# Softmax denominators in a causal latent-attention kernel: from eight fp32 transposes per query tile to a block-transposed reduction and one 16-column product

## Chip, core and metric

The kernel runs on one core of one Trainium2 chip. The metric is the device time of one execution in microseconds (us). The changed program computes the same outputs from the same inputs. Engine names are those of the profile: PE is TensorE (PEld its weight loads), DVE VectorE, ACT ScalarE, POOL GpSimd, SP the engine that issues most DMAs.

## What is computed

One sequence of 2048 tokens of width 512 goes through a latent attention with 16 heads, a residual and a layer norm, then one linear layer with a second residual and layer norm. The part that matters here, from the reference:

```python
scores = jnp.einsum('bhqd,bhkd->bhqk', q_full, k_full) * scale
scores = jnp.where(causal, -jnp.inf, scores)
attn = jax.nn.softmax(scores.astype(jnp.float32), axis=-1).astype(q_full.dtype)
out = jnp.einsum('bhqk,bhkd->bhqd', attn, v)
out = out.transpose(0, 2, 1, 3).reshape(b, s, H * DV)
return out @ w_o.T
```

The change concerns the denominator of the softmax: for every query and head the sum of the exponentials over all keys up to the query.

## The kernel before

**Tiling.** The 16 heads are four groups of four. Within a group the 2048 queries are 16 tiles of 128. That makes 64 iterations `it`, each for one group and one query tile (128 queries by 4 heads are 512 columns). Iteration `it` has `keys(it)` key tiles, 1 to 16 of them, because of causality; over all iterations there are 544. Two query tiles that lie side by side are one after the other (a pair), the one with more keys first; the pairs follow `PAIR_ORDER`, so the first iterations of a group have 14, 13, 2, 1, 16, 15, 4, 3, 12, 11, 6, 5, 8, 7, 10 and 9 key tiles.

**One key tile.** Scores are held with keys on partitions and (head, query) along the free dimension, 128x512. For each key tile:

- PE: `scores`, five 512-column matmuls (line 1464) into one of two banks;
- ACT: copy of the scores to a ring of 24 slots in SBUF (line 1606); the masked first tile is written by DVE instead (line 1847);
- DVE: running maximum `max` over the key tiles (line 1858); it releases the bank for the scores two tiles later;
- DVE: `shift` by the spread maximum (line 1873); ACT: `exp` (line 1611) and rounding to the high part `hi` (line 1618); POOL: the low part `lo` (line 1730);
- DVE: `sum`, the running sum TOTAL of the exponentials in a PSUM bank (line 1882 copies the first tile there, line 1885 adds the others);
- PE: `values`, three 512-column matmuls (lines 1494, 1495 and 1497) into the bank OUT; the third waits for `lo`.

The exponentials of a tile are handled some six slots after its scores, so the end of one iteration lies beside the scores of a later one. A slot is one `scores` and one `values` on PE.

**The end of an iteration before the change.** TOTAL holds, for each of 128 partitions, one partial sum per (head, query). ACT copies it to SBUF (`copy_sum`, line 1630), PE transposes it in four 128x128 pieces (`turn_sum`, line 1505), DVE reduces along the free dimension to 128x4 and takes the reciprocal (`reduce_sum`, lines 1889 and 1892). PE then transposes four broadcast columns, which puts the inverse of each (head, query) on all 128 partitions (`spread_sum`, line 1513). DVE multiplies the values by it (`normalise`, line 1897), ACT and POOL round the result to two parts (`o_hi` line 1636, `o_lo` line 1735), and PE multiplies by the output weights in twelve 512-column matmuls (`y`, line 1527). DVE adds that to the sum of the output (`add_y`, line 1836).

**What sets the order.** `timetable()` gives each step a slot and a phase within it, `readers()` puts the readers of a step one slot later, and `plan()` sorts them, pulling a step forward where another needs it. Every engine works through the one list `STEPS` in that order. `turn_sum`, `spread_sum`, `turn_max`, `y`, and the projections `q` and `pe` of the next pair of query tiles share three PSUM banks (`AUX`), in turns. With `e` the slot of an iteration's last values:

```python
        yield e, COPIES, ("copy_sum", it)
        yield e + 1, COPIES, ("copy_out", it)
        yield e, USE_AT, ("turn_sum", it)
        yield e + 3, USE_AT, ("spread_sum", it)
        yield e + 5, USE_AT, ("y", it)
```

The readers of `spread_sum`, which are `normalise`, `o_hi` and `o_lo`, so stand in slot e + 4, ahead of the copy of scores and of `max` of that slot. "Boundary 16" below is the end of iteration 16, and so on.

Behind iteration 58 the second layer norm and the linear layer are mixed in (lines 1535, 1547, 1902 to 1941). Ahead of the attention there is a preparation of some 150 us.

Of the kernel before, what the change touches and what calls it, by code (L numbers as in the profile page):

```python
# [15 lines left out]
P = 128  # L16
# [753 lines left out]
def timetable():  # L770

    for it in range(N_ITER):
# [55 lines left out]
def readers(use):  # L828
# [30 lines left out]

def waits_for(step):  # L860
# [9 lines left out]
    elif what == "max":  # L870
        yield ("scores", it, *rest)
        if number(it, *rest) >= RING:
            yield ("lo", *previous(it, *rest, RING))
            yield ("sum", *previous(it, *rest, RING))
# [14 lines left out]
    elif what == "sum":  # L889
        yield ("exp", it, *rest)  # L890
        if it and rest[0] == 0:
            yield ("copy_sum", it - 1)
# [10 lines left out]
    elif what == "copy_sum":  # L903
        yield ("sum", *last_tile(it))
        if it:
            yield ("turn_sum", it - 1)
# [6 lines left out]
    elif what == "turn_sum":  # L913
        yield ("copy_sum", it)
    elif what == "reduce_sum":
        yield ("turn_sum", it)
        if it >= 2:
            yield ("spread_sum", it - 2)
    elif what == "spread_sum":
        yield ("reduce_sum", it)  # L920
# [96 lines left out]
AUX_USES = ("q", "pe", "y", "turn_max", "turn_sum", "spread_sum", "turn", "linear")  # L1017
# [72 lines left out]
def attention_phase(nc, m, block, x, bias, out):  # L1090


    with ExitStack() as ctx:
# [13 lines left out]
        total = sb("total", [P, 512])  # L1107
# [5 lines left out]
        sums = sb("sums", [P, 4, HG])  # L1113
# [41 lines left out]
        sum_copied = sem("sum_copied")  # L1155
        sum_turned = sem("sum_turned")
        sum_done = sem("sum_done")
# [47 lines left out]
        def by_head(view):  # L1205

            return view.rearrange("p (h n) -> p h n", h=HG)

# [176 lines left out]
        def _(pe):  # L1385
            def wait_read(u):
# [9 lines left out]
                elif u[0] == "turn_sum":  # L1396
                    pe.wait_ge(sum_done, u[1] + 1)
# [157 lines left out]
            for what, *at in STEPS:  # L1555
# [10 lines left out]
                elif what == "turn_sum":  # L1566
                    turn_sum(*at)
                elif what == "spread_sum":
                    spread_sum(*at)
# [12 lines left out]
        def _(act):  # L1582
# [12 lines left out]
            def copy_scores(it, t):  # L1595
# [6 lines left out]
                if n >= RING:  # L1602

                    act.wait_ge(p_lo, n - RING + 1)
                    act.wait_ge(summed, n - RING + 1)
# [19 lines left out]

            def copy_sum(it):
                act.wait_ge(summed, finished(it))
                if it:
                    act.wait_ge(sum_turned, it)
                nc.scalar.copy(total[:, :], TOTAL).then_inc(sum_copied, 1)  # L1630
# [36 lines left out]
            for what, *at in STEPS:  # L1667
# [20 lines left out]
                elif what == "copy_sum":  # L1688
                    copy_sum(*at)
# [104 lines left out]
        def _(dve):  # L1794
# [80 lines left out]
            def add_up(it, t):  # L1875
                n = number(it, t)
                dve.wait_ge(exp_done, n + 1)
                if t == 0:
                    if it:

                        dve.wait_ge(sum_copied, it)
                    nc.vector.tensor_copy(TOTAL, slot(n)).then_inc(summed, 1)
                else:
# [148 lines left out]
```

## Time and profile before

| what | value |
|---|---|
| time, median of 3 runs | 1715.34 us (1714.08 to 1717.51) |
| span of the profiled execution | 1714.7 us |
| PE busy | 1679.9 us, 98% |
| PEld busy | 1395.8 us, 81% |
| DVE busy | 1380.5 us, 81% |
| ACT busy | 1120.8 us, 65% |
| POOL busy | 979.7 us, 57% |
| granted TensorE clock, mean | 0.999 |

The span runs from the first to the last instruction of one profiled execution; its own time is not recorded apart from it. The median of the runs is 0.6 us longer than the span. Busy time of an engine is the time in which at least one of its instructions is under way. Matmuls overlap, so what one costs is read from the distance between starts, not from its duration.

### The profile page before, as it was taken

Reading aid. Unit: us, or ns where it says so; the run is one execution under the profiler, and the core shown is the slowest. Engines: PE = TensorE matmul, PEld = TensorE weight load, DVE = VectorE, ACT = ScalarE, POOL = GpSimd, SP = SyncE. Lnnn points to the kernel's source line nnn. Section 1 sums busy time; section 2 is a strip of 40 time slices with the busy share of each in tenths; the row PEclk is TensorE's granted clock in tenths of the full one; section 3 lists DMA queues with packets and bytes.
Section 4 is the critical chain, followed back from the end, with each engine's and each line's share of the span. In section 5 each row is a group of like instructions: output and inputs, shape, how many; then the busy total and the mean of one; then the engine's idle time right before and its main releaser. Section 6 shows DMA issues by size and latency. Waiting matters only on the chain.

```text
span 1714.7 us, 28541 instructions
## 1 busy us (share of the span) xinstructions
PE 1679.9 (98%) x8789; PEld 1395.8 (81%) x8789; DVE 1380.5 (81%) x2493; ACT 1120.8 (65%) x2128; POOL 979.7 (57%) x937
## 2 busy tenths in 40 slices
PE   7999999999999999999999999999999999999997
PEld 5567888888888888888888888888888888888775
DVE  3665788888888887878788888888888888888984
ACT  3564676666666676666677666766667777676774
POOL 4333465565555555655566555555556665556785
PEclk9999999999999999999999999999999999999999
DMA  7984322212321412223211413123123111111422
GB/s 204 367 330 136 105 68 62 87 56 88 110 80 37 144 36 81 69 80 117 81 62 44 142 50 92 51 80 114 62 66 105 56 57 62 50 44 44 136 92 80
DMA packets 112175, 164.03 MB, mean 96 GB/s; under 512 B 13600, under 2 KB 83488, under 8 KB 109984
## 3 DMA queue, kind: packets, MB, share of 16 engines
q1 hardware_dynamic: 105296, 125.86, 22.9%
q0 software_dynamic: 4864, 16.26, 3.0%
q10 hardware_dynamic: 1872, 20.19, 2.9%
q8 instruction: 68, 1.11, 0.3%
q14 instruction: 75, 0.61, 0.1%
HBM read 101.19 MB, written 61.08 MB: 95 GB/s over the span
## 4 chain that ended last, share of the span: by engine, by line
PE 89%; POOL 3%; DVE 3%; issue 2%; DMA 1%; ACT 1%; DVEq 0%; SPq 0%; ACTq 0%; POOLq 0%
PE rows L1464 35%; PE bank L1494 7%; PE bank L1497 7%; PE bank L1495 7%; PE rows L1527 7%; PE rows L1427 5%; PE bank L1527 3%; PE rows L392 2%; PE rows L1440 2%; PE bank L1427 2%; PE bank L1484 2%; PE bank L1440 1%; POOL split_p L1730 1%; PE rows L1473 1%; PE rows L1505 1%
## 5 line engine op out<-in xcount | busy, mean ns | idle before, releaser
L1730 POOL TENSOR_TENSOR split_p<-pool,split_p 128x512 fp32r<-128x512 f32 x544 | 703.3, 1294 | 503.2 <-ACT split_p L1618 503.1
L1464 PE MATMUL rows<-q_c,key_c 128*128 128x512 f32 x1632 | 477.0, 400 | 1.4 <-DVE top L1858 1.4
L1606 ACT COPY pool<-rows 128x512 f32<-128x512 f32 x480 | 281.8, 587 | 227.3 <-PE rows L1464 226.6
L1858 DVE TENSOR_TENSOR top<-rows,top 128x512 f32<-128x512 f32 x420 | 288.6, 687 | 124.5 <-ACT pool L1606 121.0
L1873 DVE TENSOR_TENSOR pool<-bank,pool 128x512 f32<-128x512 f32 x544 | 369.7, 680 | 19.8 <-PE bank L1484 19.8
L1611 ACT ACTIVATE pool<-pool 128x512 f32<-128x512 f32 x544 | 345.9, 636 | 18.1 <-DVE pool L1873 17.1
L1618 ACT CAST split_p<-pool 128x512 fp32r<-128x512 f32 x544 | 333.2, 612 | 16.7 <-PE bank L1497 16.7
L1464 PE MATMUL rows<-q_pe,key_pe 128*128 128x512 f32 x1088 | 337.1, 391 | 0.4 <-DMA q_pe<-pe_dram 0.4
L1885 DVE TENSOR_TENSOR bank<-bank,pool 128x512 f32<-128x512 f32 x480 | 330.9, 689 | 0.0
L1464 PEld LDWEIGHTS rows<-q_c,key_c 128*128 128x128 f32 x1632 | 288.0, 189 | 50.0 <-DVE top L1858 5.0
L1464 PEld LDWEIGHTS rows<-q_pe,key_pe 128*128 128x128 f32 x1088 | 204.2, 188 | 46.2 <-DMA q_pe<-pe_dram 0.9
L1497 PE MATMUL bank<-split_p,val 128*128 128x512 f32 x544 | 213.7, 393 | 2.9 <-POOL split_p L1730 2.7
L1494 PE MATMUL bank<-split_p,val 128*128 128x512 f32 x544 | 214.0, 393 | 1.5 <-ACT o_sum L1624 1.0
L1495 PE MATMUL bank<-split_p,val 128*128 128x512 f32 x544 | 212.3, 390 | 0.0
L1527 PE MATMUL rows<-wo,o_t 128*128 128x512 f32 x528 | 127.3, 390 | 0.4 <-ACT o_t L1636 0.4
L1497 PEld LDWEIGHTS bank<-split_p,val 128*128 128x128 f32 x544 | 102.1, 188 | 29.0 <-POOL split_p L1730 7.4
L1494 PEld LDWEIGHTS bank<-split_p,val 128*128 128x128 f32 x544 | 102.1, 188 | 25.9 <-ACT o_sum L1624 3.4
L1735 POOL TENSOR_TENSOR o_t<-o_sum,o_t 128x512 fp32r<-128x512 f32 x64 | 83.0, 1296 | 69.8 <-ACT o_t L1636 69.8
L1495 PEld LDWEIGHTS bank<-split_p,val 128*128 128x128 f32 x544 | 102.2, 188 | 21.2
L1527 PEld LDWEIGHTS rows<-wo,o_t 128*128 128x128 f32 x528 | 98.9, 188 | 21.7 <-issue 1.2
L1636 ACT CAST o_t<-o_sum 128x512 fp32r<-128x512 f32 x64 | 39.7, 621 | 111.4 <-DVE o_sum L1897 97.2
L1427 PE MATMUL rows<-cq,wq 128*128 128x256 f32 x612 | 80.1, 285 | 0.3 <-DVE key_pe L611 0.3
(193 smaller groups left out, 2101.9 us busy)
## 6 DMA issues: line engine op xcount, KB each, us to landing
q_pe<-pe_dram SPq DMA_DIRECT2D x128, 128.0 KB, 2.6
y_dram<-y SPq DMA_DIRECT2D x62, 256.0 KB, 2.1
cq<-cq_dram SPq DMA_DIRECT2D x19, 768.0 KB, 4.9
y<-y_dram SPq DMA_DIRECT2D x48, 256.0 KB, 3.0
pe_dram<-by_sin SPq DMA_DIRECT2D x32, 256.0 KB, 2.1
pe_dram<-by_cos SPq DMA_DIRECT2D x32, 256.0 KB, 2.2
cq_more<-cq_dram SPq DMA_DIRECT2D x10, 768.0 KB, 4.9
table<-table_dram SPq DMA_DIRECT2D x56, 128.0 KB, 2.7
```

Of the source, the lines that this page charges most:

```text
L1464: mm = pe.matmul(by_head(out), k, q, start=(z == 0), stop=(z == 4))
L1494: pe.matmul(OUT, m.val[:, 0, j, :], split_p[:, n % 2, 0, :], start=(t == 0), stop=False)
L1495: pe.matmul(OUT, m.val[:, 1, j, :], split_p[:, n % 2, 0, :], start=False, stop=False)
L1497: pe.matmul(OUT, m.val[:, 0, j, :], split_p[:, n % 2, 1, :], start=False, stop=(t == keys(it) - 1)).then_inc(values_done, 1)
L1527: mm = pe.matmul(aux(u), o_t[:, a, h * P:h * P + P], m.wo[:, b, h, :], start=(n == 0), stop=(n == 3 * HG - 1))
L1606: nc.scalar.copy(slot(n), SCORES[n % N_SCORES]).then_inc(scores_copied, 1)
L1611: nc.scalar.activation(slot(n), slot(n), ACT.Exp).then_inc(exp_done, 1)
L1618: nc.scalar.copy(split_p[:, n % 2, 0, :], slot(n)).then_inc(p_hi, 1)
L1730: nc.gpsimd.tensor_tensor(split_p[:, n % 2, 1, :], slot(n), stored(split_p[:, n % 2, 0, :]), ALU.subtract).then_inc(p_lo, 1)
L1858: nc.vector.tensor_tensor(out, SCORES[n % N_SCORES], slot(number(it, 0)) if t == 1 else out, ALU.max).then_inc(scores_maxed, 1)
L1873: nc.vector.tensor_tensor(slot(n), MAXES, slot(n), ALU.add).then_inc(shifted, 1)
L1885: nc.vector.tensor_tensor(TOTAL, TOTAL, slot(n), ALU.add).then_inc(summed, 1)
```

## The change

The partial sums are now reduced by DVE straight from PSUM with a transposing reduction: within each block of 32 partitions by 32 columns it transposes and then sums, so 128x512 becomes 128x16 (`reduce_sum`). Each 32-partition group then holds sums over its own 32 key rows. A 128x128 matrix `fold` of repeated 32x32 identities adds the four groups in one fp32 product of 16 columns on PE (`fold_sum`). DVE takes the reciprocal of those 16 columns, and transposes them, each broadcast to 32 columns, in 32x32 blocks into the same PSUM bank, which puts the inverse of each (head, query) on all partitions (`spread_sum`, now a step of DVE). `copy_sum`, `turn_sum` and the old `spread_sum` are gone. The first exponential tile is no longer copied to TOTAL; the add of the second tile reads both. Where an iteration has one key tile, the copy stays. `fold` is built once by two DVE instructions. `spread_sum`, `normalise`, `o_hi` and `o_lo` are readers of `fold_sum`, and `y` is at e + 3.

```diff
         e = last_value(it)
         yield last_slot(it) + 1, USE_AT, ("turn_max", it)
         yield value_slot(it, 0) - 3, SPREAD, ("spread_max", it)
-        yield e, COPIES, ("copy_sum", it)
+        yield e, COPIES, ("reduce_sum", it)
         yield e + 1, COPIES, ("copy_out", it)
-        yield e, USE_AT, ("turn_sum", it)
-        yield e + 3, USE_AT, ("spread_sum", it)
-        yield e + 5, USE_AT, ("y", it)
+        yield e, USE_AT, ("fold_sum", it)
+        yield e + 3, USE_AT, ("y", it)
...
     if use[0] == "turn_max":
         return [("reduce_max", use[1])]
-    if use[0] == "turn_sum":
-        return [("reduce_sum", use[1])]
-    if use[0] == "spread_sum":
-        return [("normalise", use[1]), ("o_hi", use[1]), ("o_lo", use[1])]
+    if use[0] == "fold_sum":
+        return [("spread_sum", use[1]), ("normalise", use[1]), ("o_hi", use[1]), ("o_lo", use[1])]
...
-            def turn_sum(it):
-                u = ("turn_sum", it)
+            def fold_sum(it):
+                u = ("fold_sum", it)
                 shared(u)
-                pe.wait_ge(sum_copied, it + 1)
-                for h in range(HG):
-                    mm = pe.transpose(aux(u)[:, h * P:h * P + P], total[:, h * P:h * P + P], m.ident[:, :])
-                mm.then_inc(sum_turned, 1)
-
-            def spread_sum(it):
-                u = ("spread_sum", it)
-                shared(u)
-                pe.wait_ge(inv_done, it + 1)
-                for h in range(HG):
-                    mm = pe.transpose(aux(u)[:, h * P:h * P + P], inv_sum[it % 2][:, h:h + 1].broadcast_to([P, P]),
-                                      m.ident[:, :])
-                mm.then_inc(sum_spread, 1)
+                if it == 0:
+                    pe.wait_ge(fold_made, 2)
+                pe.wait_ge(sum_reduced, it + 1)
+                pe.matmul(aux(u)[:, 0:4 * HG], fold[:, :], row_sum[it % 2], start=True, stop=True).then_inc(sum_folded, 1)
...
-            def copy_sum(it):
-                act.wait_ge(summed, finished(it))
-                if it:
-                    act.wait_ge(sum_turned, it)
-                nc.scalar.copy(total[:, :], TOTAL).then_inc(sum_copied, 1)
...
+                if keys(it) == 1:
                     nc.vector.tensor_copy(TOTAL, slot(n)).then_inc(summed, 1)
-                else:
-                    dve.wait_ge(summed, n)
+                elif t == 1:
+                    nc.vector.tensor_tensor(TOTAL, slot(n - 1), slot(n), ALU.add).then_inc(summed, 1)
+                elif t > 1:
+                    dve.wait_ge(summed, sums_made(it, t) - 1)
                     nc.vector.tensor_tensor(TOTAL, TOTAL, slot(n), ALU.add).then_inc(summed, 1)
 
             def reduce_sum(it):
-                dve.wait_ge(sum_turned, it + 1)
-                nc.vector.tensor_reduce(row_sum[it % 2], by_head(aux(("turn_sum", it))), AX.X, ALU.add
-                                        ).then_inc(sum_done, 1)
-                dve.wait_ge(sum_done, it + 1)
-                nc.vector.reciprocal(inv_sum[it % 2], row_sum[it % 2]).then_inc(inv_done, 1)
+                dve.wait_ge(summed, sums_made(*last_tile(it)))
+                if it >= 2:
+
+                    dve.wait_ge(sum_folded, it - 1)
+                nc.vector.tensor_reduce(row_sum[it % 2], in_blocks(TOTAL), AX.X, ALU.add, apply_transpose=True
+                                        ).then_inc(sum_reduced, 1)
+
+            def spread_sum(it):
+                u = ("fold_sum", it)
+                dve.wait_ge(sum_folded, it + 1)
+                nc.vector.reciprocal(inv_sum[it % 2], aux(u)[:, 0:4 * HG]).then_inc(inv_done, 1)
+                dve.wait_ge(inv_done, it + 1)
+                nc.vector.transpose(in_blocks(aux(u)),
+                                    inv_sum[it % 2].rearrange("p (b n) -> p b n", n=1).broadcast_to([P, 4 * HG, 32])
+                                    ).then_inc(sum_spread, 1)
```

**Order on PE at boundary 16.** PE before, from the last values of iteration 16 to `y` of it; line 1464 is `scores`, lines 1494 to 1497 are `values`, line 1505 is `turn_sum`, line 1513 `spread_sum`, line 1527 `y`:

```order
1022 L1497 MATMUL bank<-split_p,val 128x512
1023 L1505 MATMUL rows<-ident,total 128x128 x4
1024 L1464 MATMUL rows<-q_c,key_c 128x512 x3
...
1038 L1497 MATMUL bank<-split_p,val 128x512
1039 L1513 MATMUL bank<-ident,sums 128x128 x4
1040 L1464 MATMUL rows<-q_c,key_c 128x512 x3
...
1049 L1497 MATMUL bank<-split_p,val 128x512
1050 L1527 MATMUL rows<-wo,o_t 128x512 x12
```

PE after, the same place (line 1513 is now `fold_sum`, line 1471 `scores`, line 1504 the last of `values`, line 1525 `y`):

```order
1006 L1504 MATMUL bank<-split_p,val 128x512
1007 L1513 MATMUL rows<-sums,fold 128x16
1008 L1471 MATMUL rows<-q_c,key_c 128x512 x3
...
1018 L1471 MATMUL rows<-q_c,key_c 128x512 x3
1019 L1471 MATMUL rows<-q_pe,key_pe 128x512 x2
...
1022 L1504 MATMUL bank<-split_p,val 128x512
1023 L1525 MATMUL rows<-wo,o_t 128x512 x12
```

Two groups of four transposes became one product of 16 columns, and `y` now stands three slots behind it instead of five: the scores of rows 1018 and 1019 are the third since the product and the last ahead of `y`.

**Order on DVE at boundary 16.** DVE before (line 1858 is `max`, 1873 `shift`, 1882 and 1885 `sum`, 1889 and 1892 `reduce_sum`, 1897 `normalise`):

```order
716 L1873 TENSOR_TENSOR pool<-bank6,pool 128x512
717 L1882 COPY bank7<-pool 128x512
718 L1858 TENSOR_TENSOR top<-rows,top 128x512
719 L1873 TENSOR_TENSOR pool<-bank6,pool 128x512
720 L1885 TENSOR_TENSOR bank7<-bank7,pool 128x512
721 L1889 TENSOR_REDUCE sums<-rows 128x4
722 L1892 RECIPROCAL sums<-sums 128x4
723 L1858 TENSOR_TENSOR top<-rows,top 128x512
...
731 L1885 TENSOR_TENSOR bank7<-bank7,pool 128x512
732 L1897 TENSOR_TENSOR o_sum<-bank4,o_sum 128x512
733 L1858 TENSOR_TENSOR top<-rows,top 128x512
```

DVE after (line 1846 is `max`, 1861 `shift`, 1871 the `sum` that joins the first two tiles, 1881 `reduce_sum`, 1887 and 1889 `spread_sum`, 1896 `normalise`):

```order
717 L1881 TENSOR_REDUCE sums<-bank 128x16
718 L1861 TENSOR_TENSOR pool<-bank,pool 128x512
719 L1846 TENSOR_TENSOR top<-rows,top 128x512
720 L1861 TENSOR_TENSOR pool<-bank,pool 128x512
721 L1871 TENSOR_TENSOR bank<-pool 128x512
722 L1887 RECIPROCAL sums<-rows 128x16
723 L1889 STREAM_TRANSPOSE rows<-sums 128x512
724 L1896 TENSOR_TENSOR o_sum<-rows,o_sum 128x512
725 L1846 TENSOR_TENSOR top<-rows,top 128x512
```

The reduction has moved up by one slot and takes the place of the copy; the transpose and `normalise` now stand where the reduction stood, both ahead of the `max` of slot e + 1.

**Order on ACT at boundary 16.** ACT after (line 1620 is `copy_out`, 1607 `exp`, 1614 `hi`, 1626 `o_hi`, 1602 the copy of scores):

```order
632 L1602 COPY pool<-rows 128x512
633 L1620 COPY o_sum<-bank 128x512
634 L1607 ACTIVATE pool<-pool 128x512
635 L1614 CAST split_p<-pool 128x512
636 L1626 CAST o_t<-o_sum 128x512
637 L1602 COPY pool<-rows 128x512
638 L1607 ACTIVATE pool<-pool 128x512
639 L1614 CAST split_p<-pool 128x512
```

`o_hi` (row 636) has moved from slot e + 4 to slot e + 1, ahead of the copy of scores (row 637) that the `max` of that slot needs; on POOL `o_lo` moves with it.

## Rows read from the trace of the kernel before

**Rows 1.** Page: span, and busy time of the engines.

```profile
span 1714.7 us, 28541 instructions
PE 1679.9 (98%) x8789; PEld 1395.8 (81%) x8789; DVE 1380.5 (81%) x2493; ACT 1120.8 (65%) x2128; POOL 979.7 (57%) x937
```

**Rows 2.** Windows: busy time (instructions) of PE, PEld, DVE, ACT, POOL; clock.

```profile
152.00:1600.00 1448.00, 1445.20 (x7595) 1225.76 (x7595) 1214.93 (x2048) 969.91 (x1798) 840.13 (x693) 1.00 0.25 79
1600.00:1714.70 114.70, 95.61 (x464) 74.48 (x462) 84.52 (x192) 70.97 (x120) 85.31 (x155) 0.98 0.24 81
```

**Rows 3.** Timeline of PE at boundary 16: start, us, instruction.

```profile
595.69 0.39 PE L1494 MATMUL bank<-split_p,val 128*128 128x512 f32 x1
...
596.37 0.60 PE L1505 MATMUL rows<-ident,total 128*128 128x128 f32 x4
596.72 0.95 PE L1464 MATMUL rows<-q_c,key_c 128*128 128x512 f32 x3
597.51 0.62 PE L1464 MATMUL rows<-q_pe,key_pe 128*128 128x512 f32 x2
597.97 0.39 PE L1494 MATMUL bank<-split_p,val 128*128 128x512 f32 x1
...
599.33 0.61 PE L1464 MATMUL rows<-q_pe,key_pe 128*128 128x512 f32 x2
...
600.47 0.84 PE L1464 MATMUL rows<-q_c,key_c 128*128 128x512 f32 x3
```

**Rows 4.** Timeline of PE in the preparation: eight short fp32 matmuls.

```profile
92.19 1.00 PE L402 MATMUL bank<-pool,x_t 128*128 128x64 f32 x8
93.03 0.61 PE L442 MATMUL bank<-ident,pool 128*128 128x128 f32 x4
```

**Rows 5.** Timeline of DVE at boundary 16.

```profile
598.15 0.69 DVE L1885 TENSOR_TENSOR bank<-bank,pool 128x512 f32<-128x512 f32 x1
598.75 0.68 DVE L1889 TENSOR_REDUCE sums<-rows 128x4 f32<-128x512 f32 x1
599.47 0.18 DVE L1892 RECIPROCAL sums<-sums 128x4 f32<-128x4 f32 x1
599.56 0.68 DVE L1858 TENSOR_TENSOR top<-rows,top 128x512 f32<-128x512 f32 x1
...
604.94 0.68 DVE L1897 TENSOR_TENSOR o_sum<-bank,o_sum 128x512 f32<-128x512 f32 x1
606.79 0.69 DVE L1858 TENSOR_TENSOR top<-rows,top 128x512 f32<-128x512 f32 x1 [1.17 <-ACT pool L1606]
```

**Rows 6.** Timeline of ACT at boundary 16.

```profile
605.65 0.62 ACT L1636 CAST o_t<-o_sum 128x512 fp32r<-128x512 f32 x1 [1.85 <-DVE o_sum L1897]
606.17 0.58 ACT L1606 COPY pool<-rows 128x512 f32<-128x512 f32 x1
```

**Rows 7.** Groups of DVE by form: count, busy us, mean ns, idle before.

```profile
L1882 DVE COPY bank<-pool 128x512 f32<-128x512 f32 x64 | 43.7, 683 | 0.0
...
L650 DVE CAST val<-c_n 128x128 f32 x16 | 3.6, 227 | 2.3 <-DVE c_n L644 0.5
```

**Rows 8.** Timelines of DVE and PE at boundary 12.

```profile
491.56 0.68 DVE L1889 TENSOR_REDUCE sums<-rows 128x4 f32<-128x512 f32 x1
...
493.74 0.84 PE L1464 MATMUL rows<-q_c,key_c 128*128 128x512 f32 x3
```

**Rows 9.** Timelines of DVE and PE at boundary 20, with a projection.

```profile
685.82 0.68 DVE L1889 TENSOR_REDUCE sums<-rows 128x4 f32<-128x512 f32 x1
...
688.36 2.39 PE L1427 MATMUL bank<-cq_more,wq 128*128 128x256 f32 x18
690.59 0.86 PE L1464 MATMUL rows<-q_c,key_c 128*128 128x512 f32 x3
```

**Rows 10.** Waits: engine, line, waited for: us in total, times, longest.

```profile
ACT o_t L1636 <- DVE o_sum L1897: 97.2, 59, 5.2
```

**Rows 11.** Groups of POOL: the low part of the exponentials.

```profile
L1730 POOL TENSOR_TENSOR split_p<-pool,split_p 128x512 fp32r<-128x512 f32 x544 | 703.3, 1294 | 503.2 <-ACT split_p L1618 503.1
```

More of the change, by code:

```diff
@@ L857, in last_tile, with sum_of, sums_made @@
     return it, keys(it) - 1
+def sum_of(it, t):
+    return it, 1 if t == 0 and keys(it) > 1 else t
+def sums_made(it, t):
+    return sum(keys(n) - (keys(n) > 1) for n in range(it)) + t + (keys(it) == 1)
 def waits_for(step):
@@ L873, in waits_for @@
             yield ("lo", *previous(it, *rest, RING))
-            yield ("sum", *previous(it, *rest, RING))
+            yield ("sum", *sum_of(*previous(it, *rest, RING)))
         if rest[0] == 1 and it >= 2:
@@ L891, in waits_for @@
         if it and rest[0] == 0:
-            yield ("copy_sum", it - 1)
+            yield ("reduce_sum", it - 1)
+        if rest[0] == 1:
+            yield ("sum", it, 0)
     elif what == "lo":
@@ L902, in waits_for @@
             yield ("o_lo", it - 2)
-    elif what == "copy_sum":
-        yield ("sum", *last_tile(it))
-        if it:
-            yield ("turn_sum", it - 1)
     elif what == "turn_max":
@@ L912, in waits_for @@
             yield ("spread_max", it - 8)
-    elif what == "turn_sum":
-        yield ("copy_sum", it)
     elif what == "reduce_sum":
-        yield ("turn_sum", it)
+        yield ("sum", *last_tile(it))
         if it >= 2:
-            yield ("spread_sum", it - 2)
+            yield ("fold_sum", it - 2)
+    elif what == "fold_sum":
+        yield ("reduce_sum", it)
     elif what == "spread_sum":
-        yield ("reduce_sum", it)
+        yield ("fold_sum", it)
     elif what == "normalise":
@@ L1016 @@
 PROJECTION_STEPS = [("q", N_PAIR - 1, 0), ("q", N_PAIR - 1, 1)]
-AUX_USES = ("q", "pe", "y", "turn_max", "turn_sum", "spread_sum", "turn", "linear")
+AUX_USES = ("q", "pe", "y", "turn_max", "fold_sum", "turn", "linear")
 def plan():
@@ L1154, in attention_phase @@
         out_copied = sem("out_copied")
-        sum_copied = sem("sum_copied")
-        sum_turned = sem("sum_turned")
-        sum_done = sem("sum_done")
+        sum_reduced = sem("sum_reduced")
+        sum_folded = sem("sum_folded")
+        fold_made = sem("fold_made")
         inv_done = sem("inv_done")
@@ L1207, in by_head, with in_blocks @@
             return view.rearrange("p (h n) -> p h n", h=HG)
+        def in_blocks(view):
+            return view.rearrange("p (b n) -> p b n", n=32)
         def by_pair(view):
@@ L1565, in _ @@
                     values(*at)
[L1566 to L1569, printed above, removed]
+                elif what == "fold_sum":
+                    fold_sum(*at)
                 elif what == "q":
@@ L1687, in _ @@
                     copy_out(*at)
-                elif what == "copy_sum":
-                    copy_sum(*at)
                 elif what == "o_hi":
@@ L1896, in normalise @@
                 dve.wait_ge(out_copied, it + 1)
-                nc.vector.tensor_tensor(o_sum[:, it % 2, :], aux(("spread_sum", it)), o_sum[:, it % 2, :], ALU.mult
+                nc.vector.tensor_tensor(o_sum[:, it % 2, :], aux(("fold_sum", it)), o_sum[:, it % 2, :], ALU.mult
                                         ).then_inc(normalised, 1)
@@ L1946, in copy_mask, with make_fold @@
                 dve.wait_ge(mask_copied, 1)
+            def make_fold():
+                nc.vector.tensor_reduce(fold[:, 0:32], m.ident[:, :].rearrange("p (a i) -> p i a", i=32), AX.X, ALU.add
+                                        ).then_inc(fold_made, 1)
+                dve.wait_ge(fold_made, 1)
+                nc.vector.tensor_copy(fold[:, 32:P].rearrange("p (a i) -> p a i", i=32),
+                                      fold[:, 0:32].rearrange("p (a i) -> p a i", a=1).broadcast_to([P, 3, 32])
+                                      ).then_inc(fold_made, 1)
             for what, *at in STEPS:
@@ L1972, in _ @@
                     reduce_sum(*at)
+                elif what == "spread_sum":
+                    spread_sum(*at)
                 elif what == "normalise":
```

15 lines of the change are left out of this document (6 added, 9 removed).

## The prediction

> **What bounds the kernel now.** I read four views in this order. The page first: PE is busy for 1679.9 of 1714.7 us, DVE for 81%, ACT for 65% [rows 1]. The windows next, to see whether that holds by stage: between 152 and 1600 us, where the attention runs, PE is idle for 1448.00 - 1445.20 = 2.8 us in all, while DVE is idle for 233 us and the granted clock is 1.00; behind 1600 us, where layer norm and linear layer are mixed in, PE is idle for 19 of 114.7 us [rows 2]. So PE sets the end, and what leaves PE is worth its full length, as long as PE finds no new wait. Then the timeline of PE, for what a group costs there, and the timelines of DVE and ACT at the same place, for how late each comes. One wait in the list of waits matters: ACT spends 97.2 us waiting for `normalise` ahead of `o_hi`, at 59 of 64 boundaries [rows 10]. It costs nothing today. The change moves exactly that wait.
>
> **What leaves PE.** Without transposes, the distance from the first `values` matmul to the fourth of the next `scores` is 599.33 - 597.97 = 1.36 us; with the four transposes of `turn_sum` it is 597.51 - 595.69 = 1.82 us [rows 3]. A group so costs 0.46 us; the five rows round to hundredths, and I take 0.45. There are 128 groups (64 `turn_sum`, 64 `spread_sum`): 57.6 us. What comes is 64 products in fp32 of 16 columns. The nearest rows are eight short fp32 matmul instructions of 64 columns, 92.19 to 93.03 us, 0.105 us each [rows 4]; the code there issues four products, so an fp32 product is two instructions. Two of them and the rounding give 0.22 us. From below the product can't be shorter than one such instruction, 0.1 us; from above, it is at most a whole group of transposes, 0.45. I take 0.22, the row it is nearest to, hence 14.4 us. PE's work falls by **43.2 us** (bounds 29 to 51).
>
> **What leaves ACT and what changes on DVE in amount.** ACT loses 64 copies of 0.59 us; they lay beside PE's work, and ACT has time to spare, so they are costed at nothing. DVE loses the copy of the first tile at 60 iterations (four have only one key tile), 0.683 us each [rows 7], and gets 64 transposes 128x512. The trace shows no DVE transpose. From below it is a plain pass over 512 columns, 0.68 us [rows 5, 7]; from above, the part that grows with the columns doubles: 128 columns take 0.227 us and 512 take 0.683 [rows 7], 0.0012 us per column, 0.61 us for 512, so 1.29 in all. I take 0.71, near the plain pass. The reduction keeps its 0.68 us for the same 512 columns, with the same upper end for its transposing form. Amounts balance within a few us, of 233 idle.
>
> The Trainium skill, page "VectorE: DVE Perf Modes", section "The three transpose paths", gives 311 ns for a DVE transpose of 128 columns in bf16. The row for a cast of 128 columns has 227 ns [rows 7], 84 ns less. By the page a transpose of 512 columns would be an estimated 0.77 us if the 84 ns are fixed, and 1.24 us if all of it grows with the columns; the sum below would rise by 1 us or by more than 10.
>
> **Where the moved steps land.** This is the term that decides. DVE issues back to back every 0.60 us (598.15 to 598.75), so three instructions per key tile, 1.80 us, nearly fill PE's 1.82 us for eight matmuls. `max` of slot e + 1 releases the bank for the scores of slot e + 3. At boundary 16 it starts at 599.56 and ends at 600.24, and those scores start at 600.47 [rows 3, 5]: 0.23 us to spare. Today one thing stands ahead of it, `reduce_sum`: 599.56 - 598.75 = 0.81 us. The late chain stands in slot e + 4: `normalise` 604.94, `o_hi` 605.65, copy of scores 606.17, `max` 606.79, 1.85 us from `normalise` to `max` [rows 5, 6]. There it does no harm, because the scores that this `max` releases come behind `y`, twelve matmuls, 2.7 us of PE.
>
> After the change the chain stands in slot e + 1 and the `max` it delays releases scores that come ahead of `y`. Counted from the end of the last `sum`'s slot (598.75): reciprocal 0.21 (0.178 and the step to a dependent instruction, as 0.68 becomes 0.72 from 598.75 to 599.47), transpose 0.71 + 0.04, `normalise` to `max` 1.85. That is 2.81 in place of 0.81: **2.0 us later**. At boundary 16 `max` would end at 602.25, the scores could start at 602.3, and PE, 0.23 us earlier through the shorter product, would want them at 600.24: a wait of 2.05 us. At boundary 12, with 493.74 - 491.56 = 2.18 us from there to the scores, against 2.81 + 0.69 + 0.06, and 0.23 again, it is 1.6 [rows 8]. Where a projection lies between, as at boundary 20 (2.2 us of PE from 688.36), scores start at 690.59, 4.77 us behind the reduction, and nothing waits [rows 9]. I laid this sum on each boundary. At 22 of 58 no projection lies between and the wait is 0.4 to 2.2 us, 1.6 on average: 0, 12 to 17, 28 to 33, 44, 45, 47, 48, 51, 52, 53, 55 and 57. At the other 36 the slack covers it; in a dozen of them less than 0.6 us is left. PE so waits **36 us**.
>
> **What is queued behind.** On ACT `exp`, `hi` of slot e + 2 stand behind the delayed copy; on POOL `lo`, 1.29 us [rows 11], behind `hi`, and `o_lo` of 1.29 us is now ahead of it. The third `values` matmul of slot e + 3 then finds its low part 0.1 to 0.2 us late at the 22, 0.6 at three where a rotation is in between, and 0.4 or so at five others: **5 us**. The transpose above one pass, and the reduction's position ahead of `shift`: 1.5 us. Two forced effects at the end: the last `y` come two slots sooner while PE idles there for waits of other steps: -1 us. PE's wait for `reduce_sum` costs nothing: it follows the last `sum` by one `max`, and `fold_sum` comes 0.5 us later; the cover is the `values` of that slot.
>
> **Sum.** -43.2 + 36 + 5 + 1.5 - 1 = -1.7 us on a span of 1714.7; with the 0.6 us from span to median, 1713.6, **1713.6 us**. The gain on PE is spent nearly whole on the new wait. A measurement of this kernel can tell some 0.2%, 3.4 us, from no change.
>
> **Rival 1: the wait is covered, the gain stays.** For it: DVE and ACT together have hundreds of us idle, and if ACT's and DVE's work of slot e + 1 starts sooner than in today's trace, because `copy_sum` is gone, the chain ends sooner. Against it: DVE is back to back from 597.5 on, without ACT in its way. If only a quarter of the 43 us of waits comes, the span is 1714.7 - 43 + 11 = 1683, and with none 1672.
>
> **Rival 2: the transposing instructions of DVE are slow, and it gets slower.** If each takes 0.6 us more, the upper end above, the transpose and the reduction put 1.2 us more on the chain of each of the 22 boundaries, 26 us, and some 0.5 us on the dozen that have less than 0.6 left, 6 us: 1713.6 + 32, a time of 1746. It decides from about 0.15 us more per instruction, where the 22 boundaries alone bring 5 us. For it: no row shows such an instruction writing to PSUM from broadcast columns. Against it: the transposeless reduction has exactly the duration of an add.
>
> **Rival 3: the product is heavier on PE**, or DVE waits for it. At the upper bound of 0.45 us it adds 64 x 0.23 = 15 us: 1728.
>
> **Chances.** The forecast's case (gain and new wait cancel, own range 1704 to 1725) 0.53; rival 1 0.17; rival 2 0.20; rival 3 0.10. Within the forecast's case about 0.19 of the 0.53 lies below 1711.9, 0.21 within 0.2% of before, 0.13 above. With rival 1 all faster, rivals 2 and 3 nearly all slower: faster 0.36, same 0.22, slower 0.42. The low end is 1686, rival 1 with a third of the waits (-43 + 14); the high end is 1742, rival 3 whole and rival 2 with nine tenths of its price. Left out are the waits that vanish wholly (about 0.1) and rival 2 at its full price (about 0.1).
>
> **What would show it.** Right: PE's busy time falls by about 40 us while its idle time between 152 and 1600 rises by about that; the waits of scores for DVE `max` or its bank appear, near 2 us each and some 20 in number; at boundary 16 `o_hi` starts 2.2 us behind the last `sum`; ACT's wait for `normalise` stays near 2 us a boundary. The transpose and the reduction read 0.7 us each, the product 0.22 us from start to start. Wrong: few waits on PE (rival 1); a transposing instruction above 0.85 us (rival 2); a product above 0.35 us (rival 3).

## The result, and the profile after

The changed kernel takes **1770.24 us** (median of 4 runs, 1767.84 to 1773.82) against 1716.42 for the kernel before on the same chip (median of 4 runs): a ratio of 1.0317, 95% interval 1.0299 to 1.0335. It is slower by 54 us. The forecast was 1713.6 with a range up to 1742: the time lies outside it. The profiled execution spans 1771.9 us, 57.2 more than that of before. First the page and the windows of the changed kernel, with the columns of [rows 1, 2].

```profile
span 1771.9 us, 27648 instructions
PE 1665.3 (94%) x8405; PEld 1365.4 (77%) x8405; DVE 1402.5 (79%) x2499; ACT 1095.1 (62%) x2064; POOL 985.2 (56%) x937
```

```profile
152.00:1600.00 1448.00, 1383.04 (x7020) 1156.99 (x7019) 1194.15 (x1982) 918.19 (x1687) 817.21 (x671) 0.99 0.24 76
1600.00:1772.00 172.00, 143.36 (x657) 112.94 (x655) 127.15 (x264) 97.11 (x167) 113.87 (x176) 0.94 0.26 85
```

PE stands idle for 1448.00 - 1383.04 = 65.0 us in the stretch where it was idle for 2.8 [rows 2]. DVE is busy for 82% of the stretch where it was 84%, so no engine took PE's place as the bound: PE waits. For what, the list of waits says (engine, line, waited for: us in total, times, longest).

```profile
ACT o_t L1626 <- DVE o_sum L1896: 119.4, 57, 3.5
...
PEld rows L1471 <- DVE top L1846: 52.3, 35, 2.7
...
PE rows L1471 <- DVE top L1846: 42.2, 34, 2.2
...
PE bank L1480 <- DVE top L1846: 12.0, 6, 2.3
...
PE bank L1513 <- DVE sums L1881: 3.9, 2, 1.9
```

ACT's wait for `normalise` grew by 22 us (119.4 us against 97.2, [rows 10]), but what matters is what stands behind it: the `max` that follows now holds PE, 42.2 us at `scores` (L1471) and 12.0 at `turn_max` (L1480). Both together were 1.7 us before. The groups of the new instructions show that none of them is slow (the two of `spread_sum` come in further groups by bank; the largest is shown):

```profile
L1881 DVE TRANSPOSE_TENSOR_REDUCE sums<-bank 128x16 f32<-128x512 f32 x64 | 45.1, 705 | 0.0
...
L1889 DVE STREAM_TRANSPOSE rows<-sums 128x512 f32<-128x512 f32 x46 | 33.4, 727 | 1.6
...
L1887 DVE RECIPROCAL sums<-rows 128x16 f32<-128x16 f32 x46 | 11.4, 248 | 0.0
```

Boundary 16, where the prediction did its sum, on DVE, ACT and PE:

```profile
612.08 0.69 DVE L1871 TENSOR_TENSOR bank<-pool 128x512 f32<-128x512 f32 x1
612.68 0.25 DVE L1887 RECIPROCAL sums<-rows 128x16 f32<-128x16 f32 x1
612.97 0.73 DVE L1889 STREAM_TRANSPOSE rows<-sums 128x512 f32<-128x512 f32 x1
613.73 0.69 DVE L1896 TENSOR_TENSOR o_sum<-rows,o_sum 128x512 f32<-128x512 f32 x1
615.59 0.69 DVE L1846 TENSOR_TENSOR top<-rows,top 128x512 f32<-128x512 f32 x1 [1.17 <-ACT pool L1602]
```

```profile
614.45 0.62 ACT L1626 CAST o_t<-o_sum 128x512 fp32r<-128x512 f32 x1 [2.06 <-DVE o_sum L1896]
614.98 0.58 ACT L1602 COPY pool<-rows 128x512 f32<-128x512 f32 x1
```

```profile
610.57 0.29 PE L1513 MATMUL rows<-sums,fold 128*128 128x16 f32 x2
610.71 0.94 PE L1471 MATMUL rows<-q_c,key_c 128*128 128x512 f32 x3
...
614.22 0.39 PE L1504 MATMUL bank<-split_p,val 128*128 128x512 f32 x1
616.34 0.96 PE L1471 MATMUL rows<-q_c,key_c 128*128 128x512 f32 x3 [1.73 <-DVE top L1846]
```

Here all went as forecast. The chain reads from left to right: `normalise` 613.73, ACT's `o_hi` 614.45, the copy of the scores behind it in ACT's queue 614.98, `max` 615.59, `scores` 616.34. PE was ready at 614.22 + 0.23 = 614.45 and waited 1.89 us, against 2.05 forecast. What was missed lies elsewhere. I walked through PE's records and compared each step from start to start with the usual one (0.227 us for 512 columns, 0.120 for 256); a step longer by over 0.25 us counts as a wait. From 150 us up to the last `values` of iteration 58:

| us | before | changed |
|---|---|---|
| last `values` of iteration 58 start at | 1599.3 | 1648.4 |
| waits at `scores` (count) | 3.0 (7) | 48.6 (35) |
| at `turn_max` | 0.5 (1) | 13.4 (7) |
| at `values` | 1.0 (2) | 7.8 (12) |
| at the product, at `spread_max`, others | 0 | 8.5 (12) |
| all waits | 4.5 | 78.4 |
| steps while the granted clock is at its low level, extra | 0 | 8.7 |
| from there to the end of the span | 115.4 | 123.5 |

Seven of the waits at `scores` lie ahead of the first boundary, 3 us in both kernels. Of the 49.1 us up to iteration 58, waits make +73.9, the clock +8.7, and the work taken from PE -39.8 (59/64 of the prediction's 43.2, an estimate). The other 6.3 are what is left over, in steps each longer by less than 0.25 us or in that estimate; these runs don't divide them. The tail adds 8.1. (The expectations below give some of these waits by another count, which took 0.8 to 2 us more at `scores`, part of it matmuls at the low clock level: 50.6 and 14.9 us there are 48.6 and 14.0 by the table's count, and 64 and 27 are 62 and 24.)

### The profile page after: what moved, and what is told of

Its sections match the earlier page's. It is cut to its first block and busy times, and to the rows that moved or that the text cites. A ratio compares the mean times of both kernels' runs of the same rounds, so it can differ in the third digit from the quotient of the medians.

```text
span 1771.9 us, 27648 instructions
## 1 busy us (share of the span) xinstructions
PE 1665.3 (94%) x8405; PEld 1365.4 (77%) x8405; DVE 1402.5 (79%) x2499; ACT 1095.1 (62%) x2064; POOL 985.2 (56%) x937
## 5 line engine op out<-in xcount | busy, mean ns | idle before, releaser
L1471 PE MATMUL rows<-q_c,key_c 128*128 128x512 f32 x1632 | 476.8, 400 | 42.7 <-DVE top L1846 42.2
L1471 PEld LDWEIGHTS rows<-q_c,key_c 128*128 128x128 f32 x1632 | 288.9, 189 | 103.7 <-DVE top L1846 52.3
L1614 ACT CAST split_p<-pool 128x512 fp32r<-128x512 f32 x544 | 332.4, 611 | 14.7 <-PE bank L1504 14.4
L1471 PE MATMUL rows<-q_pe,key_pe 128*128 128x512 f32 x1088 | 337.6, 391 | 0.0
L1874 DVE TENSOR_TENSOR bank<-bank,pool 128x512 f32<-128x512 f32 x420 | 289.6, 690 | 0.0
L1471 PEld LDWEIGHTS rows<-q_pe,key_pe 128*128 128x128 f32 x1088 | 204.5, 188 | 45.4
L1525 PE MATMUL rows<-wo,o_t 128*128 128x512 f32 x636 | 158.8, 400 | 3.0 <-DVE y L1824 3.0
L1525 PEld LDWEIGHTS rows<-wo,o_t 128*128 128x128 f32 x636 | 123.6, 195 | 29.6 <-DVE y L1824 3.4
L1504 PEld LDWEIGHTS bank<-split_p,val 128*128 128x128 f32 x544 | 102.6, 189 | 45.7 <-POOL split_p L1718 25.5
L1626 ACT CAST o_t<-o_sum 128x512 fp32r<-128x512 f32 x64 | 39.6, 619 | 147.4 <-DVE o_sum L1896 119.4
```

The lines of the kernel that those rows point to most:

```text
L1471: mm = pe.matmul(by_head(out), k, q, start=(z == 0), stop=(z == 4))
L1504: pe.matmul(OUT, m.val[:, 0, j, :], split_p[:, n % 2, 1, :], start=False, stop=(t == keys(it) - 1)).then_inc(values_done, 1)
L1525: mm = pe.matmul(aux(u), o_t[:, a, h * P:h * P + P], m.wo[:, b, h, :], start=(n == 0), stop=(n == 3 * HG - 1))
L1614: nc.scalar.copy(split_p[:, n % 2, 0, :], slot(n)).then_inc(p_hi, 1)
L1874: nc.vector.tensor_tensor(TOTAL, TOTAL, slot(n), ALU.add).then_inc(summed, 1)
```

## The experiments

The question was where the loss comes from: from the **work** that now lies on DVE, or from the **place** where the chain stands and what is queued behind it. The letters in the expectations name the theories: P is the place; W holds that the work itself is the loss, Y that it is the sooner `y`. The later letters Q, D and C are explained where they come up.

### The chain back to its old place

e1_late puts product and chain where the chain stood before, e2_y_between puts them half way.

```diff
-        yield e, USE_AT, ("fold_sum", it)
+        yield e + 3, USE_AT, ("fold_sum", it)      # e2: e + 1
-        yield e + 3, USE_AT, ("y", it)
+        yield e + 5, USE_AT, ("y", it)             # e2: e + 3, as changed
```

> The changed kernel with fold_sum at e + 3 and y at e + 5, so that its readers (spread_sum, normalise, o_hi, o_lo) stand in slot e + 4 as in the kernel before; the arithmetic stays the changed one. Theory P (place): the loss is the chain ahead of a max that releases scores ahead of y; here y lies between, so nearly all waits go and the 43 us of removed PE work show: 1672 to 1685 us. Theory W (work): the loss is in the new instructions themselves, the transposing ones on DVE, the fp32 product and the hand-overs DVE to PE to DVE; they are all still here, so it stays above 1740 us.

Measured: 1728.34 us, ratio 1.0073 (1.0056 to 1.0089). Between the two ranges: W is out, and P missed by 43 us.

> The changed kernel with fold_sum at e + 1 instead of e, y left at e + 3: the chain moves one slot down, to e + 2, and the max it delays now releases the scores of slot e + 4, which come behind y. Theory P: most waits go although y is as early as in the change, 1675 to 1695 us, a few us more than with y at e + 5, because y may meet o_lo late. Theory Y (the early y itself waits for its operands or its bank): stays above 1740 us. Theory W: above 1740 us.

Measured: 1717.39 us, ratio 1.001 (1.0 to 1.002), 22 us above P's range too, and far below what W and Y want. The timelines of ACT and PE in e1_late at boundary 16 tell why:

```profile
608.62 0.62 ACT L1626 CAST o_t<-o_sum 128x512 fp32r<-128x512 f32 x1 [2.77 <-DVE o_sum L1896]
```

```profile
608.35 0.39 PE L1504 MATMUL bank<-split_p,val 128*128 128x512 f32 x1
609.38 1.39 PE L1525 MATMUL rows<-wo,o_t 128*128 128x512 f32 x5 [0.65 <-ACT o_t L1626]
```

The waits at `scores` fall from 48.6 us to 3.1, what they were before the change. But `y` now waits for `o_hi`: it could start at 608.58 and starts at 609.38. `y` waits 25.6 us in 40 places in e1_late and 26.4 in 30 in e2. Reciprocal and transpose add about 1 us to a chain that in the kernel before just ended in time for `y` (`o_hi` at 606.27, where PE was ready for `y` at 606.38). Besides, `values` wait 13.3 us in 11 places in e1_late, most of it for `copy_out`, ACT's copy of the values (12.2 us in 8 places in the list of waits): at 362.17 and 642.54 us it stands behind an `o_hi` that waited 2.57 and 2.79 us for `normalise`. So 42 us came back by place alone, with the same instructions; P had the direction, but forgot the second end of the chain.

### The old kernel with the chain moved

Here no DVE transpose is involved; only the kernel before, with its `spread_sum` one slot sooner, `y` left (e3) or moved along (e4).

```diff
-        yield e + 3, USE_AT, ("spread_sum", it)
+        yield e + 2, USE_AT, ("spread_sum", it)
-        yield e + 5, USE_AT, ("y", it)             # e3: stays
+        yield e + 4, USE_AT, ("y", it)             # e4 alone
```

> The kernel before with spread_sum one slot sooner, at e + 2 instead of e + 3, and y left at e + 5: old arithmetic, but normalise and o_hi now delay the max of slot e + 3, whose scores come ahead of y. Theory P: slower than before though no work is added; the chain from normalise to max is 1.85 us instead of 0.6, some 0.75 us are to spare at the tight boundaries, so 0.5 to 0.9 us at 20 to 30 boundaries: 1727 to 1745 us. Theories W and Y: 1715 us, unchanged.

Measured: 1750.75 us, ratio 1.0206 (1.0189 to 1.0223): slower as P says, but 6 us above its range.

> The kernel before with spread_sum at e + 2 and y at e + 4: as the third run, but y lies between the delayed max and the scores it releases. Theory P: back to the time of before, 1711 to 1720 us. Theory Y (a sooner y costs by itself): slower than before by 5 us or more.

Measured: 1717.66 us, ratio 1.0015 (1.0005 to 1.0024), as P says. The same instructions one slot sooner cost 36 us where the delayed `max` releases scores that come ahead of `y`, and 3 where `y` comes between. Place alone makes a loss of 36 us, without any work added. In e3 the list of waits has the same rows as the changed kernel's:

```profile
PEld rows L1464 <- DVE top L1858: 28.4, 36, 1.7
...
PE rows L1464 <- DVE top L1858: 14.7, 29, 1.3
```

### The chain cut in two

Which link does it, DVE's or ACT's? e6_o_hi_late moves ACT's `o_hi` and POOL's `o_lo` three slots back and `y` two, e5_split moves `normalise` too, and e7_y_late moves only `y`, which shows what that part does alone. In e5 and e6 a bank is now held longer, so the planner must free it in a loop and keep the steps of one kind in order; that part is left out here.

```diff
-            at.setdefault((n + 1, READ), []).append(reader)
+            late = 4 if step[0] == "fold_sum" and reader[0] in ("o_hi", "o_lo") else 1   # e6
+            late = 4 if step[0] == "fold_sum" and reader[0] != "spread_sum" else 1       # e5
+            at.setdefault((n + late, READ), []).append(reader)
...
-        yield e + 3, USE_AT, ("y", it)
+        yield e + 5, USE_AT, ("y", it)              # e5, e6 and e7
```

> The change with only ScalarE's part moved: fold product, spread_sum and normalise stay in slot e+1, so that VectorE's order is the change's; o_hi and o_lo come in slot e+4, y in slot e+5. Theory Q (ScalarE's queued wait is the cause): the scores' waits for the maximum fall from 50.6 us to under 15, 1680 to 1700 us. Rival D (VectorE's own 1.7 us in that slot is the cause): they stay over 40 us, 1745 to 1765.

Measured: 1705.68 us, ratio 0.9946 (0.993 to 0.9963): faster than before by half a per cent, and 65 us below the change, yet 6 us above Q's range. Boundary 16 of this version, DVE and PE:

```profile
593.54 0.25 DVE L1897 RECIPROCAL sums<-rows 128x16 f32<-128x16 f32 x1
593.83 0.73 DVE L1899 STREAM_TRANSPOSE rows<-sums 128x512 f32<-128x512 f32 x1
594.59 0.69 DVE L1906 TENSOR_TENSOR o_sum<-rows,o_sum 128x512 f32<-128x512 f32 x1
595.20 0.68 DVE L1856 TENSOR_TENSOR top<-rows,top 128x512 f32<-128x512 f32 x1
```

```profile
595.08 0.39 PE L1514 MATMUL bank<-split_p,val 128*128 128x512 f32 x1
595.93 0.98 PE L1481 MATMUL rows<-q_c,key_c 128*128 128x512 f32 x3 [0.47 <-DVE top L1856]
```

DVE's rows are those of the change, in the same order. But `max` follows `normalise` after 595.20 - 594.59 = 0.61 us, where the change needed 615.59 - 613.73 = 1.86. The 1.25 us are the way over ACT: `o_hi`, then the copy behind it. PE's wait falls from 1.89 to 0.62 us, by the same amount, and over the run the waits at `scores` fall from 48.6 to 14.0 us. This is Q, ACT's queued wait, shown in its own terms; D wanted over 1745 us and is out as the main cause. The 14.0 us are what is left for it.

> The change with its chain cut in two: fold product and spread_sum stay in slot e+1, but normalise, o_hi and o_lo come in slot e+4, y in slot e+5 (the turned inverse waits in its bank). Theory Q (the loss is ScalarE's wait: o_hi stands in ScalarE's queue behind a chain of 1.97 us on VectorE, and the copy of the scores that the maximum reads stands behind o_hi): ScalarE no longer waits at the boundary, the scores wait no more than in the kernel before (some 6 us in all), the 40 us of TensorE saved come through: 1675 to 1695 us. Rival D (it is VectorE's own added work, 0.98 us of it still in slot e+1, that delays the maximum): about half of the 64 us of waits for the maximum stays, 1700 to 1725. Rival C (lower clock after waits is most of the loss, whatever the order): clock below 0.995 and over 1720.

Measured: 1725.99 us, ratio 1.0069 (1.0051 to 1.0088): 31 us above Q's range and just above rival D's. The waits at `scores` are 3.1 us, as before the change, so D is wrong about where. Both of rival C's signs came out, with a clock of 0.990 and a time over 1720, but the clock is not most of the loss in the change: 1 - 0.989 of its span of 1771.9 us is 19.5 us, 1 - 0.999 of 1714.7 is 1.7, so the clock can hold at most some 18 of the 57 us. In e5 itself the same sum gives some 15 us at most, and how the loss divides there stays open. What the walk shows is new: `normalise` only one slot ahead of `y` gives `y` 10.7 us of waits (13), and the bank, held for four slots, makes projections wait 8.7 us (7); its tail is 18 us longer than in the kernel before.

> The change with y alone moved back to slot e+5, where it stood in the kernel before; the chain and o_hi stay in slot e+1. Theory Q: the scores wait as in the change at the boundaries, and only the keys-4 iterations (6, 22, 38), whose cover was the y of the iteration before, get 1.5 to 2 us each back: 1755 to 1770 us. Rival Y (the loss is that y came two slots sooner, and so another order of the banks): under 1735.

Measured: 1794.01 us, ratio 1.046 (1.0443 to 1.0477): worse than the change by 24 us, and worse than I expected. Rival Y is out: y's move wasn't the loss. At iterations 6, 22 and 38 the wait of 1.90 us fell to 0.84, but the product (1.1 us at three places, 0.7 at three), `spread_max` (1.4 at three), `y` (1.4 at two) and a projection (3.3) wait anew, the tail is 7 us longer and the granted clock is 0.983 instead of 0.989. I did not take these apart further.

### Two prices

e12_twice is e6_o_hi_late with the DVE transpose made twice; e8_fold4 is e6_o_hi_late with the product made four times.

```diff
-                dve.wait_ge(inv_done, it + 1)
+                dve.wait_ge(inv_done, 2 * it + 1)
                 nc.vector.transpose(in_blocks(aux(u)),
                                     inv_sum[it % 2].rearrange("p (b n) -> p b n", n=1).broadcast_to([P, 4 * HG, 32])
+                                    ).then_inc(inv_done, 1)
+                dve.wait_ge(inv_done, 2 * it + 2)
+                nc.vector.transpose(in_blocks(aux(u)),
+                                    inv_sum[it % 2].rearrange("p (b n) -> p b n", n=1).broadcast_to([P, 4 * HG, 32])
                                     ).then_inc(sum_spread, 1)
```

> e6_o_hi_late with the turning of the inverse made twice (0.73 us more for VectorE at each of 64 boundaries, between reciprocal and normalise, ScalarE's o_hi late as in e6_o_hi_late). Theory Q with VectorE as second limit (0.98 + 0.73 us of added work are just about what a slot has free, since waits of 0.55 us are left at 27 boundaries): each further 0.73 us comes through at some 30 to 45 boundaries: 1725 to 1745 us. If VectorE had ample room once ScalarE does not wait: under 1712.

Measured: 1744.21 us, ratio 1.017 (1.0155 to 1.0186), within the range. At boundary 16 PE waits 1.39 us where e6 has 0.62: the 0.77 us of the second transpose come through whole (DVE, then PE):

```profile
603.18 0.73 DVE L1899 STREAM_TRANSPOSE rows<-sums 128x512 f32<-128x512 f32 x1
603.95 0.73 DVE L1903 STREAM_TRANSPOSE rows<-sums 128x512 f32<-128x512 f32 x1
```

```profile
604.43 0.39 PE L1514 MATMUL bank<-split_p,val 128*128 128x512 f32 x1
606.05 0.73 PE L1481 MATMUL rows<-q_c,key_c 128*128 128x512 f32 x2 [1.23 <-DVE top L1856]
```

So DVE, 82% busy over the span of e6_o_hi_late, has nothing free in this slot. Over all 64 boundaries 38.5 of 49 us came through.

```diff
+                for n in range(3):
+                    pe.matmul(aux(u)[:, 0:4 * HG], fold[:, :], row_sum[it % 2], start=True, stop=True)
                 pe.matmul(aux(u)[:, 0:4 * HG], fold[:, :], row_sum[it % 2], start=True, stop=True).then_inc(sum_folded, 1)
```

> e6_o_hi_late (1705.7 us) with the fold product of 16 columns made four times in place of once. 64 boundaries x 3 products x 0.24 us = 46 us of TensorE. If the product costs what the trace of the change shows (0.24 us from start to start) and TensorE bounds this version, less what falls into the 27 us of waits: 1735 to 1752 us. If such a product hides in TensorE's pipe and costs only its 16 columns: under 1715.

Measured: 1731.16 us, ratio 1.0091 (1.0075 to 1.0106), 4 us under the range. The timeline of PE has the three added products at one line, the last at the next:

```profile
596.82 0.73 PE L1524 MATMUL rows<-sums,fold 128*128 128x16 f32 x6
597.40 0.37 PE L1525 MATMUL rows<-sums,fold 128*128 128x16 f32 x2
597.62 0.96 PE L1481 MATMUL rows<-q_c,key_c 128*128 128x512 f32 x3
```

From the first product to the scores it is 597.62 - 596.82 = 0.80 us. With one product, in e6_o_hi_late, it is 0.14 (591.43 to 591.57). Three more so cost 0.66 us, 0.22 each and 42 us for all 64. Of that, 14 us fell into waits (24.1 to 10.1 up to iteration 58), and 25.5 came through. The product's 14.4 us in the sum were sound.

### A version that beats both

e9_three: `normalise` one slot later than in e6, in a slot of its own between `spread_sum` and `o_hi`. e11_three_tail: besides, the last two iterations as in the change. e13_best: besides, iterations 60 and 61 as in e6.

```diff
-            at.setdefault((n + 1, READ), []).append(reader)
+            late = 1
+            if step[0] == "fold_sum" and step[1] < N_ITER - 2:
+                late = {"normalise": 2 if step[1] < N_ITER - 4 else 1, "o_hi": 4, "o_lo": 4}.get(reader[0], 1)
+            at.setdefault((n + late, READ), []).append(reader)
...
-        yield e + 3, USE_AT, ("y", it)
+        yield e + (5 if it < N_ITER - 2 else 3), USE_AT, ("y", it)
```

> e6_o_hi_late with normalise one slot later still: spread_sum in slot e+1, normalise in e+2, o_hi in e+4, y in e+5. If VectorE's own work in one slot is what is left of the scores' waits (14.9 us in e6_o_hi_late), they fall to about 5 and the time to 1690 to 1700 us; if the waits come from the depth of the banks or from ScalarE, it stays at 1702 to 1709.

Measured: 1705.1 us, ratio 0.994 (0.9926 to 0.9954), no better than e6, and in the range of the other reading. By the time alone, DVE's slot would not matter. But waits at `scores` fell from 14.0 to 7.7 us and the last `values` of iteration 58 come 10.2 us sooner (1572.3 against 1582.5); the tail gives all of it back.

> e9_three, with the last two iterations' o_hi right behind their normalise and their y in slot e+3, since at the end nothing stands behind them that would wait. The stretch behind the last values of the last iteration was 3.4 us longer in e6_o_hi_late than in the kernel before: 1 to 4 us below e9_three if that is the late y, no difference if it is the order of the feed-forward part.

Measured: 1701.71 us, ratio 0.992 (0.9906 to 0.9933): 3.4 us below e9_three, as for the late `y`.

> e11_three_tail with normalise back beside spread_sum for iterations 60 and 61. In e9_three and e11_three_tail the last values of iteration 63 come 11 us behind those of iteration 62, against 6.9 us in e6_o_hi_late: there normalise(61) stands behind sum(63,0), and ScalarE's o_hi(61), with copy_out(62) behind it, waits for it. If that is the cause, the interval falls back to about 7 us and the time to 1696 to 1699 us; if it is DVE's load in the tail, it stays at 1701 to 1703.

Measured: 1697.29 us, ratio 0.9898 (0.9881 to 0.9914). The interval from the last `values` of iteration 62 to those of 63 fell from 11 to 6.8 us, as expected. ACT in e9_three, then in e13_best, at this place:

```profile
1645.98 0.62 ACT L1636 CAST o_t<-o_sum 128x512 fp32r<-128x512 f32 x1 [5.52 <-PE rows L1535]
...
1647.13 0.57 ACT L1630 COPY o_sum<-bank 128x512 f32<-128x512 f32 x1
```

```profile
1642.47 0.62 ACT L1638 CAST o_t<-o_sum 128x512 fp32r<-128x512 f32 x1 [0.55 <-PE rows L1537]
...
1643.62 0.56 ACT L1632 COPY o_sum<-bank 128x512 f32<-128x512 f32 x1
```

Again an `o_hi` that waits, here for a `y` that is late itself, with a copy that PE needs behind it. e13_best is 1.0% faster than the kernel before and 73 us faster than the change, with the same instructions as the change (27648). The windows of e13_best:

```profile
152.00:1600.00 1448.00, 1433.16 (x7338) 1205.90 (x7336) 1245.40 (x2095) 960.60 (x1767) 861.96 (x719) 1.00 0.25 80
1600.00:1696.60 96.60, 75.98 (x340) 58.73 (x338) 66.85 (x151) 52.21 (x86) 67.59 (x129) 0.93 0.25 83
```

PE is idle for 14.8 us up to 1600, not 65.0.

## Why the prediction was wrong

**The mechanism and the prices were right.** The transpose takes 0.727 us (0.71 taken), the transposing reduction 0.705 (0.68 taken), the product 0.24 from start to start (0.22 taken), the reciprocal 0.29 (0.21 taken), and boundary 16 waits 1.89 us (2.05 taken). Rivals 2 and 3 are out by these rows, rival 1 by the waits. By the Trainium skill, page "VectorE: DVE Perf Modes", section "The three transpose paths", the estimate was 0.77 or 1.24 us; the trace, with 0.727, agrees with the lower one. PE's work did fall by about the 43 us of the sum: -39.8 plus the measured change of waits gives -20.2 us up to iteration 58 for e6_o_hi_late (measured -16.8) and -28.0 for e13_best (measured -24.5). In the changed kernel PE's busy time fell by 14.6 us only, not 40. Part is the slow clock; and a matmul that ends before a wait shows its whole 0.39 us, where it otherwise lies under the next one.

**The step that failed is the count of places.** "I laid this sum on each boundary. At 22 of 58 no projection lies between": the 22 brought 36.7 us at `scores` in 19 of them, against 36 forecast. That this sum fits is in part luck: at 17, 33 and 52 no wait came, and the other 19 waited 1.9 us each where 1.6 was taken. I had looked for scores alone, as what the late `max` releases. What I missed, up to iteration 58:

- **`turn_max` reads the same `max`.** Where an iteration's scores end, no bank lies between: PE wants it at once. "At the other 36 the slack covers it", since a projection lies ahead of the scores; but `turn_max` stands ahead of the projection. PE in the changed kernel at boundary 4:

```profile
318.03 0.39 PE L1504 MATMUL bank<-split_p,val 128*128 128x512 f32 x1
320.07 0.63 PE L1480 MATMUL bank<-ident,top 128*128 128x128 f32 x4 [1.65 <-DVE top L1846]
320.45 0.72 PE L1434 MATMUL rows<-cq,wq 128*128 128x256 f32 x4
```

  At 4, 20 and 36 the wait is 1.8 us, at 8, 24 and 40 2.5 us: 13 us.
- **A cover that the change itself moved.** At boundaries 6, 22 and 38 the `y` of the iteration before had stood between; with `y` two slots sooner it is gone, and 1.9 us show. With the 0.7 us at 7, 23 and 39 and 0.3 at three others, `scores` wait 8.8 us in 9 places outside the 22 that did not wait before.
- **What follows the chain inside short iterations.** Iterations 18 and 34 have two keys: their reduction stands behind the delayed `max`, and the product waits 2.1 us for it (the fourth group of heads takes its pairs in another order, so nothing like it stands at 50) (PE):

```profile
646.83 0.39 PE L1504 MATMUL bank<-split_p,val 128*128 128x512 f32 x1
649.16 0.37 PE L1513 MATMUL bank<-sums,fold 128*128 128x16 f32 x2 [1.94 <-DVE sums L1881]
```

  With the other waits of the product, 4.8 us in all, `values` at 7.8 and `spread_max` at 3.0 this makes 15.6 us, where the sum had 5.
- **The tail.** "-1 us" for the last `y` was +8.1; with the 3.4 us that PE saves there, that is 12 us off. That the steps there wait for one another, over a chain longer by 1 us in each iteration, is my reading and not shown. The granted clock is lower there too, as the windows of the tail before and after say (0.98 and 0.93). That could be up to 6 us of it; these runs don't divide it.

```profile
1599.30:1714.70 115.40, 96.31 (x467) 75.02 (x465) 85.17 (x195) 71.61 (x121) 85.50 (x155) 0.98 0.24 81
```

```profile
1648.50:1771.90 123.40, 96.95 (x431) 74.78 (x429) 88.55 (x197) 68.96 (x115) 87.17 (x155) 0.93 0.22 73
```

- **The clock** up to iteration 58, with no term in the sum: 8.7 us, see below.

Together: waits 73.9 in place of 42.5, 31 us; tail 12; clock 9; what is left over 6. That is the whole 59 us between the forecast's span and the measured one. The range held only bounds of prices, and none of how many places there are, though that was the term that all the others were multiplied by.

My expectation for e1_late failed on the same ground: I asked who waits for `max`, not who waits for the end of the chain.

## What to carry to other kernels

When a chain is moved on an in-order queue, list everything behind it on each engine, and for each of these all its readers, not only the one that was nearest before; then ask which of the covers moves with the change. An engine that is idle for a fifth of its time can have nothing free in the one slot that counts. Where a step waits on another engine and nothing needs its result soon, put it late: the same instructions gave 1770 us with `o_hi` directly behind its producer, and 1706 with `o_hi` three slots later and `y` behind it.

## What was not expected of the hardware

In six places up to iteration 58 PE ran for a few us at its slow level, 1.2 instead of 2.4 GHz, with 0.427 instead of 0.227 us per matmul of 512 columns and 0.213 instead of 0.120 per one of 256. In the kernel before this happened nowhere in that stretch. PE behind a wait in the changed kernel, and the windows of two such places (granted clock 0.61 and 0.58):

```profile
228.63 1.45 PE L1471 MATMUL rows<-q_c,key_c 128*128 128x512 f32 x3 [1.87 <-DVE top L1846]
229.88 1.05 PE L1471 MATMUL rows<-q_pe,key_pe 128*128 128x512 f32 x2
230.73 0.63 PE L1501 MATMUL bank<-split_p,val 128*128 128x512 f32 x1
```

```profile
228.00:232.00 4.00, 3.37 (x8) 2.62 (x9) 3.98 (x7) 3.44 (x7) 3.29 (x3) 0.61 0.65 187
416.00:420.00 4.00, 3.82 (x20) 3.85 (x21) 3.62 (x7) 1.50 (x3) 3.36 (x3) 0.58 0.45 146
```

Each of the six stands right behind one of the longest waits on PE: 2.14 us at 228.6, 2.50 at 416.2, 802.2 and 1187.7 (the `turn_max` of boundaries 8, 24 and 40), 2.41 at 1514.2 and 2.23 at 1620.3. Behind two more waits of 2.41 us, at 574.9 and 960.5, and behind all the shorter ones, as at 616.34, the granted clock stayed at 1.00. Over the run it is 0.989 against 0.999 before. A wait on PE can so cost more than its length; what decides between the 2.41 us at 1514.2 and the same wait at 574.9 these runs don't settle.
